# Edge stage of a graph network kernel: where the edge attribute maximum is found, how far the attribute products trail, and how cell rows are loaded

## The chip, the cores and the metric

The kernel runs on one core of one Trainium2 chip. The metric is the device time of one execution in microseconds; lower is better. Before the change it is 3320.58 us, the median of 3 runs (3318.75 to 3322.74).

## The reference, cut to what matters

Four graph layers work on 3125 nodes with 256 features and 50000 edges, each with 64 attributes and two weights. The change touches only what prepares the edges.

```
# layer 0, with h = batch-normalised x
a_in  = segment_sum((h @ W_in  + b_in )[src] * edge_weight[:, None],    dst)
a_out = segment_sum((h @ W_out + b_out)[dst] * edge_weight_n2[:, None], src)
# layer 1, three times
e_msg = edge_attr @ We[l].T + be[l]          # edge_attr: 50000 x 64
agg   = segment_sum(x[src] + e_msg, dst) / max(deg, 1)
x     = relu(agg @ Wl[l].T + bl[l] + x @ Wr[l].T)
# layers 2 and 3 use the same edges again, by products with the count matrix
```

Two things follow from the edges alone: a 3125 x 3125 matrix of cells (edge count and the two weight sums of each source and destination pair), and the sum of the edge attributes by destination.

## The kernel before, in words

The program is written out by hand, one instruction stream for each engine, joined by counting semaphores. An engine and its DMA queue run their instructions strictly in the written order, so what stands in a stream behind a waiting instruction waits too.

The 50000 edges are 391 tiles of 128 edges, in 49 chunks of 8 tiles (EC, CH). In time the part before the cell sweep is this.

1. **Zeroing and normalisation.** SyncE writes zeros over the cell matrix in HBM (39 stores of 3000 KB, L342). Beside it x is loaded, its column statistics are found and applied (DVE L1237 to L1253), and TensorE and ScalarE make the two 256-wide feature products, 25 node tiles, while ScalarE also stores the transposed features (hT_d, L550). DVE finds the largest and smallest feature values (L1261, L1262), makes the power-of-two scales (L1268 to L1276), and ScalarE and DVE split the features into two float16 parts (L569, L1283). The semaphore feat_split tells that this is done.
2. **Duplicate search.** Two edges of a tile that fall on one cell may not both be added by one indirect DMA. So ScalarE compares each tile's cells with three rows of cells that it loads broadcast from HBM (cell_rows, L577; L587, L595), 12 tiles ahead (AHEAD). TensorE decides which edge claims a cell (claim, L860) and adds up the values (sums, L870 to L875). DVE writes values and row numbers of a chunk (values, L1303 to L1306).
3. **Scatter.** For each tile GpSimd issues one indirect DMA that adds the values to the cell matrix (L505). It needs the whole matrix zeroed and the chunk's values ready; before the issue for tile t it waits for the landing of tile t-2. The values sit in VALS = 6 buffers.
4. **Attribute products.** For each tile DVE writes a one-hot of the destinations, 128 x 3125 in float16 (one_hot, L1318), into one of 3 buffers, and TensorE makes seven 500-column products with it (attributes, L884). The attributes are loaded by chunk (L361) and split into two float16 parts (attr_hi, attr_low). For the split their largest value must be known: 13 loads of 960 KB and a small one into two buffers, each read by two reductions of DVE (L1335, L1336), then a scale.

The tight loop of the last three runs in slots, one a tile (`for t in range(ET + LAG)` and its DVE and ACT counterparts). In slot t tile t is claimed and tile t - LAG has its attribute products, with LAG = EC * LAG_C, 48 slots before the change. The attribute maximum stands in DVE's stream at slot 37 (PEAK_SLOT) and its loads in SyncE's stream behind the zeroing and behind feat_split. The store of the normalised x (h_d, L353) also stands there, since the attribute chunks are loaded over its place in SBUF.

When the last scatter has landed (landed, L366) and the attribute sums are read out (s_ready), SyncE loads the first cells of the sweep (L373). From there on the change touches nothing.

Of the kernel before, what the change touches and what calls it, by code (L numbers as in the profile page):

```python
# [28 lines left out]
def build_gnn(nc, x, src, dst, edge_attr, edge_w, edge_w2, gamma0, beta0, W_in, b_in, W_out, b_out, W_x2i, b_x2i,  # L29
# [3 lines left out]
    E, EA = edge_attr.shape  # L33
# [22 lines left out]

    LAG_C = 6
    LAG = EC * LAG_C
    VALS = 6
    AHEAD = EC + 4  # L60
    PEAK_LOADS = 13
    PEAK_TILES = EM // PEAK_LOADS
    PEAK_SLOT, SCALE_SLOT = 37, 38

# [24 lines left out]
    with ExitStack() as ctx:  # L89
# [3 lines left out]
        def sem(name):  # L93
            return ctx.enter_context(nc.semaphore(name))
# [180 lines left out]
        peak_in = [sem(f"peak_in{s}") for s in range(2)]  # L275
        attr_in = [sem(f"attr_in{s}") for s in range(2)]
        landed = [sem(f"landed{s}") for s in range(2)]
        cells_in = [sem(f"cells_in{s}") for s in range(3)]
# [56 lines left out]
        def _(sp):  # L335
# [8 lines left out]

            sp.wait_ge(S["feat_split"], 2 * PIECES)
            for i in range(PEAK_LOADS):
                if i >= 2:
                    sp.wait_ge(S["peak_read"], i - 1)
                sp.dma_start(peak_buf[i % 2].rearrange("p (t a) -> p t a", a=EA), attr_main[:, i * PEAK_TILES:(i + 1) * PEAK_TILES, :]).then_inc(peak_in[i % 2], 16)
            sp.wait_ge(S["peak_read"], PEAK_LOADS - 1)  # L350
            sp.dma_start(peak_buf[PEAK_LOADS % 2][0:TAIL, 0:EA], edge_attr[EM * 128:E, :]).then_inc(peak_in[PEAK_LOADS % 2], 16)
            for lo, hi in ((0, K0), (K0, P)):
                sp.dma_start(by_node(h_d)[lo:hi], Xn[lo:hi]).then_inc(S["h_kept"], 16)  # L353
            sp.wait_ge(S["h_kept"], 32)
            for c in range(CH):
                if c >= 2:
                    sp.wait_ge(S["attr_lo"], c - 1)
                else:
                    sp.wait_ge(S["scale_a_ready"], 1)
# [110 lines left out]
        def _(pool):  # L470
# [21 lines left out]
            for q in (0, 32, 64):  # L492
                row = lambda b: brow[q + b:q + b + 1, 0:D]
                for a, v in ((row(0), b_in), (brow[q:q + 1, D:2 * D], b_out), (brow[q + 1:q + 2, :], b_x2i),
                             (row(2), bl[0]), (row(3), bl[1]), (row(4), bl[2]), (row(5), b_post)):
                    pool.dma_start(a, r1(v)).then_inc(S["bias_in"], 16)

            pool.wait_ge(S["zeroed"], 16 * (3 * CELLS // SLAB))
            for t in range(ET):
# [18 lines left out]
        def _(act):  # L518
# [53 lines left out]
            def load_rows(c):  # L572
                if c >= 2:
                    act.wait_ge(S["abs_done"], EC * (c - 1))
                a, b = max(EC * c - 1, 0), min(EC * c + EC + 1, ET)
                i_ = a - (EC * c - 1)
                act.dma_start(rows[c % 2][:, i_:i_ + b - a], cell_rows[a:b, :].unsqueeze(0).to_broadcast([128, b - a, 128])).then_inc(rows_in[c % 2], 16)  # L577
            for c in range(2):
                load_rows(c)

            def distance(t):
                c, k = divmod(t, EC)
                if k == 0:
                    act.wait_ge(rows_in[c % 2], 16 * (c // 2 + 1))
# [18 lines left out]
            def attr_hi(c):  # L603
                act.wait_ge(attr_in[c % 2], 16 * (c // 2 + 1) + (16 if c == CH - 1 else 0))
# [180 lines left out]
        def _(pe):  # L785
# [63 lines left out]
            pe.wait_ge(S["tr_read"], TR_AT["peak"])  # L849
            pe.matmul(trp[:, 0, 0:2], ident[0:1, 0:1].to_broadcast([1, 128]), power2[0:1, :], start=True, stop=True).then_inc(S["tr_done"], 1)  # L850

            def claim(t):
# [34 lines left out]
            for t in range(ET + LAG):  # L887
                if t == SCALE_SLOT + 1:
                    pe.wait_ge(S["tr_read"], TR_AT["peak2"])
                    pe.wait_ge(S["peak_a_ready"], 1)  # L890
                    pe.transpose(trp[0:1, 0, 0:128], peak_a, ident[:, :]).then_inc(S["tr_done"], 1)
                    pe.wait_ge(S["tr_read"], TR_AT["peak_a"])
                    pe.matmul(trp[:, 1, 0:1], ident[0:1, 0:1].to_broadcast([1, 128]), power_a[0:1, :], start=True, stop=True).then_inc(S["tr_done"], 1)
# [256 lines left out]
        def _(dve):  # L1150
# [103 lines left out]
            dve.wait_ge(S["stat"], 3)  # L1254

            for g in range(PIECES):
                dve.wait_ge(S["nat_ready"], NAT_AT["feat", (g + 1) * ROWS - 1])
# [18 lines left out]
            link(dve.tensor_scalar(scale0[:, 1:2], scale0[:, 1:2], ROOM, None, ALU.mult))  # L1276
            dve.sem_inc(S["scale0_ready"], 1)

            for n in range(2 * PIECES):
# [41 lines left out]
            for t in range(ET + LAG + EC):  # L1321
# [7 lines left out]
                if k == 5 and 1 <= c <= CH:  # L1329
                    values(c - 1)  # L1330
                if t == PEAK_SLOT:
                    for i in range(PEAK_LOADS + 1):
                        dve.wait_ge(peak_in[i % 2], 16 * (i // 2 + 1))
                        n, v = (128, peak_buf[i % 2]) if i < PEAK_LOADS else (TAIL, peak_buf[i % 2][0:TAIL, 0:EA])
                        dve.tensor_reduce(peaks_a[0:n, 0, i:i + 1], v, AX.X, ALU.max)  # L1335
                        last = dve.tensor_reduce(peaks_a[0:n, 1, i:i + 1], v, AX.X, ALU.min)  # L1336
                        last.then_inc(S["peak_read"], 1)
                    dve.wait_ge(S["peak_read"], PEAK_LOADS + 1)
                    link(dve.tensor_scalar(peaks_a[:, 1], peaks_a[:, 1], -1.0, None, ALU.mult))
                    dve.tensor_reduce(peak_a, peaks_a, AX.XY, ALU.max).then_inc(S["peak_a_ready"], 1)  # L1340
                if t == SCALE_SLOT:
                    dve.wait_ge(S["tr_done"], TR_AT["peak_a"])
                    dve.tensor_reduce(power_a[0:1, :], trp[0:1, 0, 0:128], AX.X, ALU.max).then_inc(S["tr_read"], 1)
                    dve.wait_ge(S["tr_done"], TR_AT["peak_a2"])
                    dve.tensor_scalar(power_a, trp[:, 1, 0:1], 2.0 ** -60, 2.0 ** 60, ALU.max, ALU.min).then_inc(S["tr_read"], 1)
                    dve.wait_ge(S["tr_read"], TR_AT["peak_a2"])
                    link(dve.tensor_scalar(power_a.bitcast(I32), power_a.bitcast(I32), 0x7F800000, None, ALU.bitwise_and))
                    link(dve.tensor_scalar(scale_a.bitcast(I32), power_a.bitcast(I32), -1.0, float(254 << 23), ALU.mult, ALU.add))
                    dve.tensor_scalar(unscale_a, power_a, 2.0 ** -14, None, ALU.mult)
                    link(dve.tensor_scalar(scale_a, scale_a, 2.0 ** 14, None, ALU.mult))  # L1350
                    dve.sem_inc(S["scale_a_ready"], 1)

# [240 lines left out]
```

## Time and profile before

| | |
|---|---|
| median of 3 runs | 3320.58 us |
| span of the profiled execution | 3315.2 us |
| median over the span of the profile | 5.4 us |
| zeroing of the cell matrix ends, first scatter | 352.66 us |
| first one-hot | 435.32 us |
| last scatter issued | 1183.19 us |
| first cell load of the sweep | 1243.72 us |

The times in the lower four lines count from the start of the span. PE is TensorE, ACT is ScalarE, POOL is GpSimd, SP is SyncE; an engine name with a q (SPq, ACTq) is the issue of DMAs by it. A releaser (`<-`) is what ended an idle time.

### The profile page before, as it was taken

To read this page: it belongs to the slowest core of one execution; us is meant where nothing else is said; L and a number is where in the kernel's file an instruction comes from. 1 tells how busy PE (TensorE), PEld (TensorE's weight loads), DVE (VectorE), ACT (ScalarE), POOL (GpSimd) and SP (SyncE) were. 2 spreads that over 40 slices of the span, in tenths; PEclk is the share of its full clock that TensorE was granted. 3 is DMA by queue.
4 is the path that set the end of the run, shared out by engine and by line. 5 is a ranking of instruction groups with operands and counts; after the bars stand their busy time and mean duration, and the time that the engine had idled before them with its cause. 6 is when DMAs were issued, how large, how long until landed. Compare 5 with 4: busy or idle time off the path is not lost. (4 is left out here: it accounts for less than half of the span.)

```text
span 3315.2 us, 37002 instructions
## 1 busy us (share of the span) xinstructions
PE 2562.0 (77%) x14593; PEld 1400.3 (42%) x14593; DVE 1677.6 (51%) x1848; ACT 1262.7 (38%) x2535; POOL 803.3 (24%) x611
## 2 busy tenths in 40 slices
PE   0551067777777777888888697998999978989896
PEld 0320033333333334444444443555555654555543
DVE  2540679999999994555545444102122242133313
ACT  0137067777777406666666422001011111122203
POOL 3000567777777722222222100000000000000000
PEclk9885589999999999999999898999999988999897
DMA  9999843333333309888898534534434424454362
GB/s 376 402 389 409 241 81 57 57 57 57 57 57 57 32 10 234 216 217 218 214 233 212 138 68 90 115 82 95 106 78 99 91 67 99 100 123 105 77 142 68
DMA packets 326008, 466.24 MB, mean 141 GB/s; under 512 B 106089, under 2 KB 261992, under 8 KB 325604
## 3 DMA queue, kind: packets, MB, share of 16 engines
q1 hardware_dynamic: 246445, 420.30, 46.9%
q0 software_dynamic: 57360, 0.92, 4.9%
q10 hardware_dynamic: 22023, 42.59, 4.0%
q8 instruction: 117, 1.92, 0.3%
q14 instruction: 63, 0.52, 0.1%
HBM read 313.97 MB, written 149.75 MB: 140 GB/s over the span
## 5 line engine op out<-in xcount | busy, mean ns | idle before, releaser
L1034 PE MATMUL psum<-FR 125*128 125x500 f16 (+1 forms) x4200 | 825.3, 355 | 40.9 <-DVE FR L1534 20.8
L505 POOL DMA_INDIRECT cell_mat<-ROW x391 | 619.6, 1585 | 536.3 <-DMA cell_mat<-SA 323.8
L884 PE MATMUL psum<-AR,Q 128*128 128x500 f16 (+1 forms) x2737 | 592.5, 356 | 184.0 <-DVE AR L1318 174.1
L1318 DVE TENSOR_SCALAR AR<-Q,ROW 128x3125 f16<-128x3125 f16 x391 | 721.4, 1902 | 7.0 <-PE psum L884 0.5
L1034 PEld LDWEIGHTS psum<-FR 125*128 125x128 f16 x4200 | 388.1, 98 | 451.8 <-issue 68.6
L884 PEld LDWEIGHTS psum<-AR,Q 128*128 128x128 f16 x2737 | 237.2, 98 | 455.5 <-DVE AR L1318 175.0
L1450 DVE SCALAR_TENSOR_TENSOR Q<-psum,small,ROW 128x1000 f32<-128x1000 f32 (+1 forms) x42 | 48.2, 1147 | 747.3 <-PE psum L1034 747.3
L1383 DVE SCALAR_TENSOR_TENSOR Q<-Q,small 125x1000 f16<-125x1000 f32 (+1 forms) x175 | 248.1, 1421 | 263.5 <-ACT Q L654 263.2
L654 ACT ACTIVATE Q<-Q,small 125x1000 f16<-125x1000 f32 (+1 forms) x175 | 262.2, 1499 | 116.7 <-DMA Q<-cell_mat 116.0
L928 PE MATMUL psum<-Q,FR 125*128 125x500 f16 (+1 forms) x1050 | 238.4, 365 | 77.9 <-DVE Q L1383 76.0
L982 PE MATMUL psum<-wl,Q 128*125 128x256 f32 (+1 forms) x1100 | 286.8, 401 | 5.7 <-ACT Q L700 3.0
L514 POOL CAST Q<-Q 125x500 f16<-125x500 f32 (+1 forms) x175 | 155.6, 890 | 550.2 <-DMA Q<-cell_mat 543.0
L587 ACT ACTIVATE AR<-AR,ROW 128x384 bf16<-128x384 f32 x391 | 235.0, 601 | 11.0 <-DMA AR<-cell_rows 10.6
L914 PE MATMUL psum<-Q,FR 125*128 125x500 f16 (+1 forms) x1050 | 210.7, 356 | 22.4 <-ACT Q L645 14.2
L982 PEld LDWEIGHTS psum<-wl,Q 128*125 128x125 f32 x1100 | 197.7, 188 | 62.4 <-issue 25.5
L645 ACT ACTIVATE Q<-psum 125x1000 f16<-125x1000 f16 (+1 forms) x175 | 159.8, 913 | 125.1 <-PE psum L914 95.5
L595 ACT ACTIVATE AR<-AR 128x384 bf16<-128x384 bf16 x391 | 198.7, 508 | 0.0
L627 ACT ACTIVATE ROW<-psum 128x1 f32<-128x1 f32 x391 | 64.9, 166 | 300.3 <-PE psum L860 289.4
L688 ACT ACTIVATE Q<-psum 128x1000 f32<-128x1000 f32 (+1 forms) x35 | 32.0, 915 | 377.1 <-PE psum L1061 377.1
L928 PEld LDWEIGHTS psum<-Q,FR 125*128 125x128 f16 x1050 | 91.9, 101 | 173.8 <-DVE Q L1383 89.8
L914 PEld LDWEIGHTS psum<-Q,FR 125*128 125x128 f16 x1050 | 93.8, 98 | 123.0 <-ACT Q L645 24.9
L629 ACT ACTIVATE ROW<-SA,ROW 128x9 bf16<-128x9 bf16 x391 | 119.1, 305 | 12.7
(271 smaller groups left out, 2321.4 us busy)
## 6 DMA issues: line engine op xcount, KB each, us to landing
cell_mat<-SA SPq DMA_DIRECT2D x39, 3000.0 KB, 31.7
Q<-cell_mat SPq DMA_DIRECT2D x150, 703.1 KB
FR<-count_mat SPq DMA_DIRECT2D x180, 585.9 KB
AR<-cell_rows ACTq DMA_DIRECT2D x47, 640.0 KB
count_mat<-Q SPq DMA_DIRECT2D x150, 117.2 KB
AR<-in_edge_attr SPq DMA_DIRECT2D x13, 960.0 KB, 4.7
Q<-in_edge_attr SPq DMA_DIRECT2D x48, 256.0 KB
cell_mat<-ROW POOLq DMA_INDIRECT x391
```

The lines of the kernel that those rows point to most:

```text
L505: pool.indirect_dma_start(out=cell_mat, out_offset=bass.IndirectOffsetOnAxis(ap=at[c % VALS][:, k:k + 1], axis=0), in_=vals[c % VALS][:, k ...
L587: act.activation(apart[t % 2].rearrange("p (j n) -> p j n", j=3), rows[c % 2][:, k:k + 3], ACT.Abs, bias=cell_neg[:, t:t + 1]).then_inc(S[ ...
L595: act.activation(same[c % 3][:, k], apart[t % 2].rearrange("p (j n) -> p j n", j=3), ACT.Relu, bias=1.0, scale=-1.0).then_inc(S["eq_done"], 1)
L645: act.activation(outw[:, 0:nt, :, tt * P:(tt + 1) * P], turn[n % 2][:, 0:nt], ACT.Copy).then_inc(S["turned"], 1)
L654: act.activation(split[n % 3][:, 0, :, 0:w], cells[n % 3][:, 0:3 * w].rearrange("p (n c) -> p c n", c=3)[:, 1:3], ACT.Copy, scale=scale0[0 ...
L884: last = pe.matmul(a, own_attr, onehot[t % 3][:, t0:t0 + nt], start=t == 0, stop=t == ET - 1, skip_group_check=True)
L914: last = pe.matmul(out_acc[:, hh, 0:ws], feat[1][:, t0 + k, c, f], outw[:, k, d, 0:ws], start=k == 0 and q == 0, stop=k == nt - 1 and q == ...
L928: pe.matmul(in_acc[:, hh, 0:w], feat[0][:, t, c, f], split[n % 3][:, d, 0, 0:w], start=t == 0 and q == 0, stop=t == NT - 1 and q == 2, ski ...
L982: last = pe.matmul(o, a[:, k * P:(k + 1) * P], wt, start=q == 0, stop=bias is None and q == len(ops) - 1)
L1034: last = pe.matmul(a[:, hh, 0:w], parts[:, c, t, f], slot(m, j)[:, i_, :], start=t == 0 and c == 0, stop=t == NT - 1 and c == 1, skip_grou ...
L1318: dve.tensor_scalar(onehot[t % 3], iota16, dst_c[:, t:t + 1], None, ALU.is_equal).then_inc(S["onehot_ready"], 1)
L1383: dve.scalar_tensor_tensor(out=split[n % 3][:, 1, :, 0:w], in0=cells[n % 3][:, 0:3 * w].rearrange("p (n c) -> p c n", c=3)[:, 1:3], scalar ...
```

## The change

It has five parts.

- The attribute maximum moves in DVE's stream from slot 37 to a place ahead of the feature maxima, right behind the input normalisation; its two buffers move from AR to FR. The scale that follows from it is made right behind the feature scales. ScalarE waits for the last of these reads before it writes the second half of the split features, which share FR.
- The 14 loads of the maximum, the store of h_d and the first 7 attribute chunk loads (EARLY) move from SyncE's stream to GpSimd's, ahead of the first scatter. SyncE keeps chunks 7 to 48, behind the zeroing. Chunk c from 2 on waits until chunk c-2 is split.
- LAG_C goes from 6 to 1: the attribute products trail the claims by 8 slots instead of 48.
- VALS goes from 6 to 14.
- Each chunk's cell rows come in three loads of 4, 3 and 3 rows (ROW_PARTS), issued at k = 1, 3 and 5 of the chunk before, instead of one load of 10 at k = 1.

```diff
-    LAG_C = 6
+    LAG_C = 1
-    VALS = 6
+    VALS = 14
-    PEAK_SLOT, SCALE_SLOT = 37, 38
+    EARLY = 7
+    ROW_PARTS = ((0, 4), (4, 7), (7, 10))
...
-        peak_buf = [AR[:, s * PEAK_TILES * EA:(s + 1) * PEAK_TILES * EA] for s in range(2)]
+        peak_buf = [FR[:, 6600 + s * PEAK_TILES * EA:6600 + (s + 1) * PEAK_TILES * EA] for s in range(2)]
... SyncE: these go
-            sp.wait_ge(S["feat_split"], 2 * PIECES)
-            for i in range(PEAK_LOADS):
...
-                sp.dma_start(by_node(h_d)[lo:hi], Xn[lo:hi]).then_inc(S["h_kept"], 16)
-            sp.wait_ge(S["h_kept"], 32)
-            for c in range(CH):
+            for c in range(EARLY, CH):
+                sp.wait_ge(S["attr_lo"], c - 1)
... GpSimd, ahead of the scatters
+            for i in range(PEAK_LOADS):
+                if i >= 2:
+                    pool.wait_ge(S["peak_read"], i - 1)
+                pool.dma_start(peak_buf[i % 2].rearrange("p (t a) -> p t a", a=EA), attr_main[:, i * PEAK_TILES:(i + 1) * PEAK_TILES, :]).then_inc(peak_in[i % 2], 16)
...
+            pool.wait_ge(S["feat_split"], 2 * PIECES)
+            for lo, hi in ((0, K0), (K0, P)):
+                pool.dma_start(by_node(h_d)[lo:hi], Xn[lo:hi]).then_inc(S["h_kept"], 16)
+            pool.wait_ge(S["h_kept"], 32)
+            for c in range(EARLY):
+                if c >= 2:
+                    pool.wait_ge(S["attr_lo"], c - 1)
+                pool.dma_start(attr32[c % 2], attr_main[:, EC * c:EC * c + EC, :]).then_inc(early_in[c % 2], 16)
... ScalarE
+                if n == PIECES:
+                    act.wait_ge(S["peak_read"], PEAK_LOADS + 1)
...
-                if k == 1 and 0 <= c + 1 < CH and c:
-                    load_rows(c + 1)
+                if k in (1, 3, 5) and c and c + 1 < CH:
+                    load_rows(c + 1, k // 2)
```

The streams show where things stand. First GpSimd's stream before, from the last bias row on (brow: bias rows; cell_mat<-ROW: the scatters; Q<-Q: casts of the sweep).

```order
L496 DMA brow<-in_L_gnn_bl 1x16x16 x3
L496 DMA brow<-in_L_gnn_b_post 1x16x16
L505 DMA cell_mat<-ROW 9984000x3 x391
L514 CAST Q<-Q 125x500 x150
L514 CAST Q<-Q 125x125 x25
```

And the same place now.

```order
L485 DMA brow<-in_L_gnn_b_post 1x16x16
L490 DMA FR<-in_edge_attr 128x1920 x13
L492 DMA FR<-in_edge_attr 80x64
L495 DMA h_d<-Q 120x25x256
L495 DMA h_d<-Q 5x25x256
L500 DMA Q<-in_edge_attr 128x512 x7
L509 DMA cell_mat<-ROW 9984000x3 x391
```

Twenty-three DMAs stand ahead of the first scatter; the last nine of them wait for feat_split, and of these five also for the split of earlier attribute chunks.

Next DVE's stream where the claims begin. Before (L1294: the mask of earlier edges; L1303 to L1306: values of a chunk; L1335: the first read for the attribute maximum):

```order
L1283 SCALAR_TENSOR_TENSOR FR<-AR,small,FR 125x5x256 x10
L1287 MEMSET AR 128x128
L1294 TENSOR_TENSOR Q<-AR,ROW 128x1024 x2
L1303 TENSOR_REDUCE ROW<-ROW 128x24
L1304 SCALAR_TENSOR_TENSOR ROW<-ROW 128x8
L1305 TENSOR_TENSOR ROW<-ROW 128x8
L1306 TENSOR_TENSOR ROW<-ROW 128x8
L1294 TENSOR_TENSOR Q<-AR,ROW 128x1024
```

Now (L1342: the split of an attribute chunk; L1348: one-hots):

```order
L1313 SCALAR_TENSOR_TENSOR FR<-AR,small,FR 125x5x256 x10
L1317 MEMSET AR 128x128
L1324 TENSOR_TENSOR Q<-AR,ROW 128x1024
L1342 SCALAR_TENSOR_TENSOR Q<-Q,small 128x8x64
L1324 TENSOR_TENSOR Q<-AR,ROW 128x1024
L1348 TENSOR_SCALAR AR<-Q,ROW 128x25x125 x5
L1342 SCALAR_TENSOR_TENSOR Q<-Q,small 128x8x64
L1348 TENSOR_SCALAR AR<-Q,ROW 128x25x125
L1333 TENSOR_REDUCE ROW<-ROW 128x24
```

The second instruction of the loop now needs the first attribute chunk, and one-hots begin before the values of chunk 0 are written.

## Rows read from the trace of the kernel before

**Rows 1.** Page, costliest groups of instructions: busy us, mean ns | idle before.

```profile
L505 POOL DMA_INDIRECT cell_mat<-ROW x391 | 619.6, 1585 | 536.3 <-DMA cell_mat<-SA 323.8
L1318 DVE TENSOR_SCALAR AR<-Q,ROW 128x3125 f16<-128x3125 f16 x391 | 721.4, 1902 | 7.0 <-PE psum L884 0.5
```

**Rows 2.** Stretches: window, length, busy PE, PEld, DVE, ACT, POOL, clock, DMA share, GB/s.

```profile
250.00:300.00 50.00, 6.54 (x97) 4.56 (x97) 4.05 (x12) 43.06 (x122) 0.00 (x0) 0.50 1.02 409
350.00:400.00 50.00, 0.00 (x0) 0.00 (x0) 42.39 (x21) 0.00 (x0) 32.58 (x21) 0.50 0.72 194
600.00:700.00 100.00, 76.37 (x528) 38.92 (x528) 98.70 (x85) 70.83 (x206) 75.60 (x47) 1.00 0.37 57
```

**Rows 3.** Timeline of the edge stage: start, us, engine, what [idle before <-releaser].

```profile
352.66 1.69 POOL L505 DMA_INDIRECT cell_mat<-ROW  x1 [323.76 <-DMA cell_mat<-SA]
409.04 9.15 SPq L353 DMA_DIRECT2D h_d<-Q  x2
429.59 4.64 SPq L361 DMA_DIRECT2D Q<-in_edge_attr  x3
432.37 0.72 ACT L610 ACTIVATE Q<-Q,small 128x512 f16<-128x512 f32 x1 [11.17 <-DMA Q<-in_edge_attr]
435.32 3.71 DVE L1318 TENSOR_SCALAR AR<-Q,ROW 128x3125 f16<-128x3125 f16 x2
1183.19 1.55 POOL L505 DMA_INDIRECT cell_mat<-ROW  x1 [0.30 <-issue]
1243.72 2.34 SPq L373 DMA_DIRECT2D Q<-cell_mat  x6
```

**Rows 4.** Stretches of the scatters alone (L505), then of the last values (L1306).

```profile
604.60:1108.20 503.60, 382.24 (x240) 1.00 0.36 56
1108.20:1184.80 76.60, 60.28 (x39) 1.00 0.29 19
...
615.10:1113.80 498.70, 5.04 (x30) 1.00 0.36 56
```

**Rows 5.** Timeline of one chunk's scatters and its cell row load.

```profile
612.01 2.02 POOL L505 DMA_INDIRECT cell_mat<-ROW  x1 [0.30 <-issue]
614.34 1.55 POOL L505 DMA_INDIRECT cell_mat<-ROW  x1 [0.30 <-issue]
617.50 1.54 POOL L505 DMA_INDIRECT cell_mat<-ROW  x1 [1.62 <-DMA cell_mat<-ROW]
...
612.16 0.33 ACTq L577 DMA_DIRECT2D AR<-cell_rows  x1
```

**Rows 6.** Start of the program: timeline of PE, then of DVE.

```profile
72.34 1.97 PE L799 MATMUL psum<-ident,AR 128*128 128x128 f32 x8 [54.15 <-DMA AR<-in_L_gnn_We]
133.67 6.82 DVE L1253 TENSOR_TENSOR Q<-Q,FR 125x6400 f32<-125x6400 f32 x1
229.17 0.17 DVE L1264 TENSOR_SCALAR small<-small 125x10 f32<-125x10 f32 x1
248.71 0.17 DVE L1287 MEMSET AR<- 128x128 f32 x1
```

**Rows 7.** Groups by line, DVE, windows 0:400 (first) and 140:250.

```profile
L1335 DVE TENSOR_REDUCE small<-AR 128x1 f32<-128x1920 f32 x11 | 23.7, 2152 | 45.2 <-DMA AR<-in_edge_attr 44.9
...
L1261 DVE TENSOR_REDUCE small<-AR 125x1 f32<-125x1280 f32 x10 | 14.8, 1481 | 60.3 <-ACT AR L560 60.3
```

**Rows 8.** DMA, window 60:80: packets, MB, share by queue (q1 SyncE, q10 ScalarE).

```profile
q1 hardware_dynamic: 1687, 6.61, 80.1%
q10 hardware_dynamic: 1687, 1.66, 23.5%
```

**Rows 9.** DMA issues, windows 0:352 and 350:412: KB each, us from issue to landing.

```profile
cell_mat<-SA SPq DMA_DIRECT2D x39, 3000.0 KB, 31.7
FR<-in_L_gnn_gamma POOLq DMA_DIRECT2D x1, 125.0 KB, 6.9
...
AR<-in_edge_attr SPq DMA_DIRECT2D x11, 960.0 KB, 4.7
```

More of the change, by code:

```diff
@@ L276, in build_gnn @@
         attr_in = [sem(f"attr_in{s}") for s in range(2)]
+        early_in = [sem(f"early_in{s}") for s in range(2)]
         landed = [sem(f"landed{s}") for s in range(2)]
@@ L496, in _ @@
                     pool.dma_start(a, r1(v)).then_inc(S["bias_in"], 16)
+            for i in range(PEAK_LOADS):
+                if i >= 2:
+                    pool.wait_ge(S["peak_read"], i - 1)
+                pool.dma_start(peak_buf[i % 2].rearrange("p (t a) -> p t a", a=EA), attr_main[:, i * PEAK_TILES:(i + 1) * PEAK_TILES, :]).then_inc(peak_in[i % 2], 16)
+            pool.wait_ge(S["peak_read"], PEAK_LOADS - 1)
+            pool.dma_start(peak_buf[PEAK_LOADS % 2][0:TAIL, 0:EA], edge_attr[EM * 128:E, :]).then_inc(peak_in[PEAK_LOADS % 2], 16)
+            pool.wait_ge(S["feat_split"], 2 * PIECES)
[6 more added lines that the diff above has]
+                pool.dma_start(attr32[c % 2], attr_main[:, EC * c:EC * c + EC, :]).then_inc(early_in[c % 2], 16)
             pool.wait_ge(S["zeroed"], 16 * (3 * CELLS // SLAB))
@@ L568, in _, with load_rows @@
                 now = slice(g * ROWS, (g + 1) * ROWS)
+                if n == PIECES:
+                    act.wait_ge(S["peak_read"], PEAK_LOADS + 1)
                 act.activation(feat[b][:, now, 0], Bn[b][:, now], ACT.Copy, scale=scale0[0:P, 0:1]).then_inc(S["feat_hi"], 1)
             act.wait_ge(S["feat_split"], 2 * PIECES)
-            def load_rows(c):
+            def load_rows(c, part):
                 if c >= 2:
                     act.wait_ge(S["abs_done"], EC * (c - 1))
-                a, b = max(EC * c - 1, 0), min(EC * c + EC + 1, ET)
-                i_ = a - (EC * c - 1)
-                act.dma_start(rows[c % 2][:, i_:i_ + b - a], cell_rows[a:b, :].unsqueeze(0).to_broadcast([128, b - a, 128])).then_inc(rows_in[c % 2], 16)
+                first = EC * c - 1
+                a, b = max(first + ROW_PARTS[part][0], 0), min(first + ROW_PARTS[part][1], ET)
+                act.dma_start(rows[c % 2][:, a - first:b - first], cell_rows[a:b, :].unsqueeze(0).to_broadcast([128, b - a, 128])).then_inc(rows_in[c % 2], 16)
             for c in range(2):
-                load_rows(c)
+                for part in range(len(ROW_PARTS)):
+                    load_rows(c, part)
             def distance(t):
@@ L583, in distance @@
                 if k == 0:
-                    act.wait_ge(rows_in[c % 2], 16 * (c // 2 + 1))
+                    act.wait_ge(rows_in[c % 2], 16 * len(ROW_PARTS) * (c // 2 + 1))
                 if t >= 2:
@@ L603, in attr_hi @@
             def attr_hi(c):
-                act.wait_ge(attr_in[c % 2], 16 * (c // 2 + 1) + (16 if c == CH - 1 else 0))
+                if c < EARLY:
+                    act.wait_ge(early_in[c % 2], 16 * (c // 2 + 1))
+                else:
+                    act.wait_ge(attr_in[c % 2], 16 * len(range(EARLY + (c - EARLY) % 2, c + 1, 2)) + (16 if c == CH - 1 else 0))
                 if c >= 2:
@@ L850, in _ @@
             pe.matmul(trp[:, 0, 0:2], ident[0:1, 0:1].to_broadcast([1, 128]), power2[0:1, :], start=True, stop=True).then_inc(S["tr_done"], 1)
+            pe.wait_ge(S["tr_read"], TR_AT["peak2"])
+            pe.wait_ge(S["peak_a_ready"], 1)
+            pe.transpose(trp[0:1, 0, 0:128], peak_a, ident[:, :]).then_inc(S["tr_done"], 1)
+            pe.wait_ge(S["tr_read"], TR_AT["peak_a"])
+            pe.matmul(trp[:, 1, 0:1], ident[0:1, 0:1].to_broadcast([1, 128]), power_a[0:1, :], start=True, stop=True).then_inc(S["tr_done"], 1)
             def claim(t):
@@ L887, in _ @@
             for t in range(ET + LAG):
[L888 to L893, printed above, removed]
                 if 1 <= t <= ET:
@@ L1254, in _ @@
             dve.wait_ge(S["stat"], 3)
+            for i in range(PEAK_LOADS + 1):
+                dve.wait_ge(peak_in[i % 2], 16 * (i // 2 + 1))
+                n, v = (128, peak_buf[i % 2]) if i < PEAK_LOADS else (TAIL, peak_buf[i % 2][0:TAIL, 0:EA])
+                dve.tensor_reduce(peaks_a[0:n, 0, i:i + 1], v, AX.X, ALU.max)
+                last = dve.tensor_reduce(peaks_a[0:n, 1, i:i + 1], v, AX.X, ALU.min)
+                last.then_inc(S["peak_read"], 1)
+            dve.wait_ge(S["peak_read"], PEAK_LOADS + 1)
+            link(dve.tensor_scalar(peaks_a[:, 1], peaks_a[:, 1], -1.0, None, ALU.mult))
+            dve.tensor_reduce(peak_a, peaks_a, AX.XY, ALU.max).then_inc(S["peak_a_ready"], 1)
             for g in range(PIECES):
@@ L1277, in _ @@
             dve.sem_inc(S["scale0_ready"], 1)
+            dve.wait_ge(S["tr_done"], TR_AT["peak_a"])
+            dve.tensor_reduce(power_a[0:1, :], trp[0:1, 0, 0:128], AX.X, ALU.max).then_inc(S["tr_read"], 1)
+            dve.wait_ge(S["tr_done"], TR_AT["peak_a2"])
+            dve.tensor_scalar(power_a, trp[:, 1, 0:1], 2.0 ** -60, 2.0 ** 60, ALU.max, ALU.min).then_inc(S["tr_read"], 1)
+            dve.wait_ge(S["tr_read"], TR_AT["peak_a2"])
+            link(dve.tensor_scalar(power_a.bitcast(I32), power_a.bitcast(I32), 0x7F800000, None, ALU.bitwise_and))
+            link(dve.tensor_scalar(scale_a.bitcast(I32), power_a.bitcast(I32), -1.0, float(254 << 23), ALU.mult, ALU.add))
+            dve.tensor_scalar(unscale_a, power_a, 2.0 ** -14, None, ALU.mult)
+            link(dve.tensor_scalar(scale_a, scale_a, 2.0 ** 14, None, ALU.mult))
+            dve.sem_inc(S["scale_a_ready"], 1)
             for n in range(2 * PIECES):
@@ L1330, in _ @@
                     values(c - 1)
[L1331 to L1351, printed above, removed]
             dve.wait_ge(S["attr_done"], ET)
```

10 lines of the change are left out of this document (removed).

## The prediction

> **What bounds the kernel now.** I read the page's groups first, then the stretches, then the timelines of the edge stage. The two costliest groups outside the layers are GpSimd's scatters and DVE's one-hots [rows 1]; both belong to the stage ahead of the cell sweep. The stretches show three phases [rows 2]. Until 352.66 the DMA engines are full (share 1.02 in 250:300) while DVE has 4 us of work in 50. In 350:400 DVE reads the attributes for their maximum, PE and ACT do nothing. From 435 on DVE is busy 98.7 us of 100, in one chunk of 8 slots every 16.62 us (30 chunks in 498.7 us [rows 4]), 2.077 us a slot. The stage's end is set by DVE: the first one-hot starts at 435.32, the last scatter is issued at 1183.19, and the sweep's first cell load comes only at 1243.72, when the attribute sums are out [rows 3]. So 60 us of slack separate the scatters from the end.
>
> A second bound lies close behind. The scatters take 240 issues in 503.6 us, 2.098 us each [rows 4], a hair slower than DVE's 2.077: GpSimd has values waiting and goes at its own pace. An issue costs 1.55 + 0.30 = 1.85 us; the rest is once a chunk, beside the cell row load of 612.16: one issue of 2.02 instead of 1.55, and an idle of 1.62 until the scatter two back has landed [rows 5]. In the last 39, with little other traffic (19 GB/s against 56), it is 76.6/39 = 1.96 [rows 4].
>
> **Start of the claims (first part).** The maximum is read right after DVE's normalisation, which ends at 133.67 + 6.82 = 140.5 [rows 6]. The first two loads now run beside the weight loads that PE waits for until 72.34 [rows 6]. With two queues at work each gets the same number of packets, 1687 and 1687 in 20 us [rows 8]; per engine that is 105 rounds, 190 ns a round, and (6.61 + 1.66) MB/20 us = 26 bytes/ns an engine. A load of 960 KB is 128 partition rows of 7680 B, 8 per engine. Two loads put 16 packets of 295 ns ahead of the weights: +5 us, DVE is ready at 145.
>
> One load under the zeroing takes 8 rounds of (4000 + 7680)/26 = 449 ns, 3.6 us and a fixed part: gamma, 8 packets of 1000 B an engine, landed in 6.9 us on this very queue, and its rounds make 1.5 [rows 9], so 5 us. That is 8.6 us against 4.7 without the zeroing [rows 9]. Both buffers turn in 8.6 + two reductions of 2.15 with 0.3 for hand-over, 13.1 us for two loads [rows 7]. The thirteenth is read by 145 + 4.3 + 6 x 13.1 = 228. Then 20 feature reductions of 1.48 [rows 7], at most 30 us, 28 as each starts before the last is through: the feature maxima are done at 257 instead of 229.2. From there to the split's end it took 19.5 us before (229.17 to 248.71 [rows 6]), and the attribute scale adds 2.5: 279. The 28 us are paid under the zeroing, by nobody but the claims.
>
> **Store of h_d and first attribute chunk (second part).** Chunk 0 may only come when h_d is stored. The store has 3000 packets of 1 KB on 15 engines, 200 each; it was issued at 409.04 and SyncE, which waited for it, went on at 429.59; less the fixed part some 17 us of data, 84 ns a packet, with only scatters beside it [rows 3]. Beside zeroing each packet waits for one of 4000 B, 154 ns: 200 x 238 = 48 us, or 200 x 193 = 39 us if bytes alone count. I take 43, and 5 fixed: 327. GpSimd must also write 3000 descriptors; from the 128 of a scatter in 1.55 us that is at most 12 ns each, 36 us, and hides in the transfer; laid end to end it would cost 30 more. Chunk 0 lands 7 us later (8 rounds of 233 ns and 5), at 334. ACT's attr_hi to the first one-hot took 3 us (432.37 to 435.32 [rows 3]); with the four slots still to claim I take 7: **first one-hot at 341**, 94 us earlier. The claims stand still at slot 3 from about 285 to 334, and no longer run 36 slots ahead under the zeroing. That is the price of LAG 8, and the reason that not all of the time gets through.
>
> **DVE's path.** From slot 8 on nothing leaves DVE's work: the same 391 one-hots and 49 masks and splits. 391 slots of 2.077 = 812 us: attribute sums out at 341 + 812 + 3 = 1156. Values of the last chunk (slot 397) at 341 + 389 x 2.077 = 1149, seven scatters of 1.85 and a landing of about 3: 1166.
>
> **GpSimd's path (second and fourth part).** The zeroing ended at 352.66 with the engines full. 12.8 MB for the maximum at 409 GB/s [rows 2] are 31 us, h_d 10 to 17, seven attribute loads 4.5: 402. GpSimd's last early load (chunk 6) waits for the split of chunk 4 in slot 36, 341 + 28 x 2.077 = 399. Both let the scatters start at 402. VALS = 14 holds 112 tiles; at 402 DVE has written 24, so it doesn't bind.
>
> **Cell rows in three (fifth part).** A load of 640 KB becomes 256, 192 and 192. Per chunk of 8 issues the ideal is 14.8 us and the actual one 16.79; 2.0 us are the row and attribute loads' doing. The stall is what a load delays a landing beyond its slack of about 0.7 us, so smaller pieces hide better: I take 0.5 for the first part, which meets the attribute load, and 0.1 for the others. The longer issue (up to 0.47) came when ACT's issue met the start of GpSimd's; with three issues a chunk I take 3 x 0.17 = 0.5, and 0.15 of rest. 14.8 + 1.25 = 16.05 a chunk, **2.00 a tile**. Ends: 1.88 (nothing left but traces) and 2.10 (no gain). ACT's new limit, the third part landing before the next chunk's first comparison three slots later (6.2 us), isn't reached: even the whole 640 KB had let the scatters go 5.3 us after its issue [rows 5]. A miss would cost each chunk what lies beyond 6.2.
>
> GpSimd: 402 + 391 x 2.00 + 3 = **1187**. That is later than DVE's 1166, and so the new end.
>
> **A rule against the move.** Scatters take 1.55 us beside a DVE that is 98.7% busy with one-hots, and 1.54 at 617.50 as well as 1.69 at 352.66 before any one-hot [rows 2, 3, 5]. By the Trainium skill (SBUF — State Buffer, Who interferes with whom) a DVE instruction in a two-port mode locks GpSimd out, and a DMA issued from GpSimd then waits for its descriptors; moving 23 DMAs there would make each wait for up to a one-hot, 1.9 us. By that rule six early loads would cost at most 11 us of GpSimd's time; the trace doesn't show it for scatters, and the reads of the maximum are reductions.
>
> **The sum.** The first cell load goes from 1243.7 to 1187, -57. PE now idles some 40 us ahead of the sweep instead of 10; at 350:400 an idle PE stood at clock 0.50 [rows 2], so the first tiles run slow: +2. Nothing later moves. 3315.2 - 55 = 3260 of the profiled execution; the median lay 5.4 above its span, so 3265.
>
> **The rivals.**
> - *DVE stays the bound.* The three loads hide fully, the pace is under 1.95, and DVE's 1166 decides: -77, 3245. For it: 1.85 in every undisturbed stretch. Against: three issues a chunk instead of one, and 1.96 in the nearly undisturbed tail. 20%.
> - *The split of the row loads does nothing.* The bytes are the same and the pace stays 2.10: 402 + 821 + 3 = 1226, -16 with the clock, 3305. The same time results if h_d is late by 30 and the pace 2.02. 22%.
> - *GpSimd's queue starves beside the zeroing (slower).* The place is the 13 loads of the maximum. I have no row of a large load on this queue; a store of the zeroing takes 31.7 us to land [rows 9]. If a load takes that, two turn in 36.3: the maximum at 367, features split at 418, and with the zeroing over by then h_d needs 22: first one-hot at 455. The scatters can't start before slot 36, at 513, and end at 513 + 782 + 3 = 1298: +54, 3375. The point from which it is slower is a first one-hot after 397, that is 18 us a load instead of 8.6. Against it: the 31.7 hold several stores queued behind each other, and gamma landed in 6.9. 8%.
> - *The change does not take the maximum off the path*: DVE reads it while it would idle anyway, but h_d and the attributes come out so late that the first one-hot is at 390 to 400: within 0.2%. 4%.
>
> My forecast, GpSimd bound with a pace of 1.95 to 2.06: 46%. For a range of 8 in 10: 3238 (DVE bound, h_d by bytes) to 3312 (old pace and 6 us more). 0.2% is 6.6 us, about what a measurement of this kernel can tell. Faster: 46 + 20 + 21 = 87%; same 5%; slower 8%.
>
> **What would show it.** Right: first one-hot near 341; first scatter near 402, released by the zeroing; mean spacing 2.00 with landing waits under 1 us; first cell load near 1187 with DVE done some 30 us before. Wrong: reads of the maximum more than 7 us apart a load; GpSimd waiting for values rather than landings at the end (DVE bound); a first scatter released by an attribute load well after 402; DVE below 98% busy in the loop, which would mean rows or attributes come late.

## The result, and the profile after

The changed kernel takes 3291.58 us, the median of 4 runs (3289.40 to 3295.41), against 3321.66 (3318.75 to 3322.76, 4 runs) of the kernel before: a ratio of 0.9913, 95% interval 0.9901 to 0.9925. The forecast was 3265 with a range of 3238 to 3312. The sign, the range and the bound that was named (GpSimd) held; the pace of the scatters did not get better as forecast, and the gain is 30 us, where 56 were forecast.

The profiled execution is the longest of the four, 3295.41 us, with a span of 3293.4. First its two groups from the page (busy, mean ns | idle before), which answer to [rows 1], then the edge stage's timeline, put together by engine: GpSimd, DVE, PE, SyncE (start, us, what [idle before <-releaser]), which answers to [rows 3, 6].

```profile
L1348 DVE TENSOR_SCALAR AR<-Q,ROW 128x3125 f16<-128x3125 f16 x391 | 722.4, 1902 | 9.2 <-PE psum L899 1.5
L509 POOL DMA_INDIRECT cell_mat<-ROW x391 | 610.4, 1561 | 211.4 <-DMA cell_mat<-ROW 110.8
```

```profile
281.80 2.32 POOL L495 DMA_DIRECT2D h_d<-Q  x2 [57.45 <-DVE FR L1313]
313.92 1.16 POOL L500 DMA_DIRECT2D Q<-in_edge_attr  x2 [29.81 <-DMA h_d<-Q]
...
388.56 0.54 POOL L500 DMA_DIRECT2D Q<-in_edge_attr  x1 [16.08 <-DVE Q L1342]
397.18 1.68 POOL L509 DMA_INDIRECT cell_mat<-ROW  x1 [8.08 <-DMA cell_mat<-SA]
...
1209.30 1.55 POOL L509 DMA_INDIRECT cell_mat<-ROW  x1 [0.30 <-issue]
...
139.02 6.82 DVE L1262 TENSOR_TENSOR Q<-Q,FR 125x6400 f32<-125x6400 f32 x1
...
230.79 2.14 DVE L1269 TENSOR_REDUCE small<-FR 128x1 f32<-128x1920 f32 x1
...
261.51 0.17 DVE L1283 TENSOR_SCALAR small<-small 125x10 f32<-125x10 f32 x1
...
281.59 0.17 DVE L1317 MEMSET AR<- 128x128 f32 x1
...
326.04 3.71 DVE L1348 TENSOR_SCALAR AR<-Q,ROW 128x3125 f16<-128x3125 f16 x2
...
1142.51 0.34 DVE L1364 TENSOR_SCALAR SA<-psum,small 128x125 f32<-128x125 f32 x1
...
1223.53 1.09 PE L948 MATMUL psum<-ident,Q 125*125 125x125 f16 x8 [82.23 <-DVE Q L1392]
...
1213.86 2.44 SPq L362 DMA_DIRECT2D Q<-cell_mat  x6
```

Read it from the end. DVE has put the attribute sums out at 1142.9; the last scatter is issued at 1209.30, and the first cell load at 1213.86, where it was 1243.72: 29.9 us earlier. (The medians differ by 30.1, but the spans of these two profiles only by 21.8: behind the first cell load the changed one takes 8.0 us more. The part on the sweep below comes back to that.) GpSimd now ends the stage, DVE 66 us ahead of it. The first one-hot came 109 us earlier than before, the last scatter 26 us later: the kernel before had 60 us between last scatter and first cell load, the changed one has 4.6.

Where the scatters' time goes shows in GpSimd's waits between 450 and 1130, first of the kernel before and then of the changed one (what it waited for: us, times, longest). A landing wait is idle time of GpSimd that ends when an earlier scatter has landed (`<- DMA cell_mat<-ROW`).

```profile
POOL cell_mat L505 <- issue: 83.6, 264, 1.2
POOL cell_mat L505 <- DMA cell_mat<-ROW: 80.4, 62, 3.3
```

```profile
POOL cell_mat L509 <- DMA cell_mat<-ROW: 101.8, 87, 2.6
POOL cell_mat L509 <- issue: 74.3, 236, 1.2
```

The "issue" part is the fixed 0.30 us between two issues. The rest is waiting for the landing of the scatter two back: shorter at the worst (2.6 for 3.3 us) but in 87 places instead of 62, and in sum more. Each landing wait holds the fixed 0.30 us too; above it they are 101.8 - 87 x 0.30 = 75.7 us, where the kernel before had 80.4 - 62 x 0.30 = 61.8. One place looks like this (GpSimd's scatters, then ScalarE's loads of cell rows, then SyncE's load of attributes), beside [rows 5]:

```profile
702.90 1.56 POOL L509 DMA_INDIRECT cell_mat<-ROW  x1 [0.34 <-issue]
704.77 1.55 POOL L509 DMA_INDIRECT cell_mat<-ROW  x1 [0.30 <-issue]
708.29 1.55 POOL L509 DMA_INDIRECT cell_mat<-ROW  x1 [1.97 <-DMA cell_mat<-ROW]
...
703.62 0.33 ACTq L583 DMA_DIRECT2D AR<-cell_rows  x1
707.81 0.33 ACTq L583 DMA_DIRECT2D AR<-cell_rows  x1
...
704.10 0.33 SPq L350 DMA_DIRECT2D Q<-in_edge_attr  x1
```

and the attribute load of the kernel before that belongs to [rows 5]:

```profile
612.64 0.33 SPq L361 DMA_DIRECT2D Q<-in_edge_attr  x1
```

The load of 703.62 is the first of its chunk, 256 KB, and the attribute load of another 256 KB goes out 0.5 us behind it. The landing wait that follows is 1.97 us, where the whole 640 KB of 612.16, with its attribute load also 0.5 us behind it, had 1.62 [rows 5]. So the smaller first piece doesn't make this wait shorter. The second load, at 707.81, is followed by none.

### The profile page after: what moved, and what is told of

The parts are those of the page before. It is cut to its first block and busy times, and to the rows that moved or that the text cites. A ratio compares the mean times of both kernels' runs of the same rounds, so it can differ in the third digit from the quotient of the medians.

```text
span 3293.4 us, 37092 instructions
## 1 busy us (share of the span) xinstructions
PE 2569.1 (78%) x14593; PEld 1405.8 (43%) x14593; DVE 1676.6 (51%) x1848; ACT 1267.4 (38%) x2535; POOL 805.8 (24%) x634
## 5 line engine op out<-in xcount | busy, mean ns | idle before, releaser
L1348 DVE TENSOR_SCALAR AR<-Q,ROW 128x3125 f16<-128x3125 f16 x391 | 722.4, 1902 | 9.2 <-PE psum L899 1.5
L509 POOL DMA_INDIRECT cell_mat<-ROW x391 | 610.4, 1561 | 211.4 <-DMA cell_mat<-ROW 110.8
L948 PE MATMUL psum<-ident,Q 125*125 125x125 f16 x1250 | 104.2, 226 | 82.2 <-DVE Q L1392 82.2
L937 PEld LDWEIGHTS psum<-Q,FR 125*128 125x128 f16 x1050 | 93.0, 102 | 172.6 <-DVE Q L1392 88.0
L948 PEld LDWEIGHTS psum<-ident,Q 125*125 125x125 f16 x1250 | 101.8, 143 | 112.4 <-issue 85.3
```

Of the source, the lines that this page charges most:

```text
L509: pool.indirect_dma_start(out=cell_mat, out_offset=bass.IndirectOffsetOnAxis(ap=at[c % VALS][:, k:k + 1], axis=0), in_=vals[c % VALS][:, k ...
L937: pe.matmul(in_acc[:, hh, 0:w], feat[0][:, t, c, f], split[n % 3][:, d, 0, 0:w], start=t == 0 and q == 0, stop=t == NT - 1 and q == 2, ski ...
L948: last = pe.transpose(turn[n % 2][:, k, c], split[n % 3][:, c, 1, k * P:(k + 1) * P], ident16[0:P, 0:P])
L1348: dve.tensor_scalar(onehot[t % 3], iota16, dst_c[:, t:t + 1], None, ALU.is_equal).then_inc(S["onehot_ready"], 1)
```

## The experiments

The theory after the result: the stage ends with GpSimd's scatters, DVE's path is free by 66 us, and the pace fell short because three row loads a chunk disturb more scatters than one. Rivals: DVE still decides, through the values; the lag or the early loads brought the gain; the attribute loads hold the scatters up; the missing microseconds lie in the cell sweep.

All paces below are counted in one window, 520 to 1070, in which every kernel scatters all the time. The view is the stretch 520:1070 with the scatters' line alone (length, busy, count, clock, DMA share, GB/s).

**One row load a chunk again.** Run twice, the second time on the same chip as a repeat of the changed kernel.

```diff
-    ROW_PARTS = ((0, 4), (4, 7), (7, 10))
+    ROW_PARTS = ((0, 10),)
-                if k in (1, 3, 5) and c and c + 1 < CH:
+                if k == 1 and c and c + 1 < CH:
```

> The changed kernel with one row load a chunk (10 rows) instead of three. Changed kernel: 320 scatters beside the loads took 684 us, 2.137 us each, the last 70 1.86. Theory of the prediction (smaller pieces hide): the pace goes back to 2.20 or more, the time rises by 15 to 30 us. Rival 1 (a load costs a stall whatever its size): the pace falls to 2.10 or below, the time falls by 8 to 15 us. Rival 2 (only the bytes count): pace and time stay within 3 us.

> The changed kernel with one row load a chunk, a second time, on the same chip as the changed kernel itself. The pace of the scatters was 2.086 with one load against 2.136 with three, 264 x 0.05 = 13 us less for the middle of the run, of which 6 us were seen in the median. Theory that three loads cost: 4 to 8 us below the changed kernel again. Rival (spread of the runs): no difference.

> The changed kernel unchanged, to compare with on the same chip: 3290 to 3293 us, pace 2.13 to 2.14.

Measured: 3285.68 us (3276.35 to 3290.03), ratio 0.9886 (0.9868 to 0.9904); again 3286.45, 0.9898 (0.9881 to 0.9915). The changed kernel repeated: 3291.56, 0.9914 (0.9897 to 0.9931). The first cell load stands at 1206.81 and 1204.24, against 1213.86 and 1216.00. In the window 264 scatters instead of 259 (first the changed kernel, then one row load):

```profile
520.00:1070.00 550.00, 404.12 (x259) 1.00 0.39 57
```

```profile
520.00:1070.00 550.00, 424.08 (x264) 1.00 0.37 57
```

With one load the issues are longer (424.08/264 = 1.61 us against 404.12/259 = 1.56), as [rows 5] had shown, but the landing waits between 450 and 1130 are only 68.7 us in 55 places:

```profile
POOL cell_mat L509 <- issue: 87.3, 273, 1.7
POOL cell_mat L509 <- DMA cell_mat<-ROW: 68.7, 55, 2.5
```

ScalarE's queue between 450 and 1130 (packets, MB, share of the engines), first of the changed kernel, then with one load:

```profile
q10 hardware_dynamic: 16416, 24.78, 13.9%
```

```profile
q10 hardware_dynamic: 5472, 24.78, 11.1%
```

The bytes are the same 24.78 MB, the packets a third. The split of the row loads costs 5 to 6 us both times. The intervals of the two kernels' ratios still overlap, but in the second comparison, on one chip, all four times with one load (the highest 3288.59) lie below all five of the changed kernel (the lowest 3289.31), and the counts of scatters and the place of the first cell load say the same. **The change without the split is the fastest complete kernel here**, level with its two variants further below (3286.38 and 3286.98).

Which of the three loads costs it can be counted from GpSimd's timeline. Each landing wait above 0.30 between 520 and 1070 (33 chunks) is put down to the row load that was issued last before the wait began. In the changed kernel that makes 1.2 us a chunk behind the first load (with the attribute load beside it), 0.1 behind the second and 0.7 behind the third, 2.0 in all (1.1, 0.1 and 0.7 in its repeat); with one load it is 1.4, in the kernel before 1.5.

**Five row loads a chunk.**

```diff
+    ROW_PARTS = ((0, 2), (2, 4), (4, 6), (6, 7), (7, 10))
+                if 1 <= k <= 5 and c and c + 1 < CH:
+                    load_rows(c + 1, k - 1)
```

> The changed kernel with five row loads a chunk (2, 2, 2, 1 and 3 rows) at k = 1 to 5. The same bytes in more pieces. Prediction's theory: pace under 2.10, time down by 10 us or more. A stall for each load: pace 2.2 or more, time up by 20 us or more. Bytes alone: no change.

Measured: 3292.08 us, ratio 0.9911 (0.9896 to 0.9926); 258 scatters in the window, first cell load 1217.36; the landing waits 114.1 us in 121 places. From three to five loads the scatters hardly get slower. The landing waits look as if they went on growing, from 101.8 us, but 34 more places hold the fixed 0.30 us each, 10.2 us, which stood under "issue" before; above it they are 77.8 us against 75.7. Both theories that expected 10 us or 20 us of change are out; "bytes alone" fits this pair, but not the step from one load to three.

**The kernel before with three row loads.** The row loads' part of the change alone.

> The kernel before with three row loads a chunk instead of one, nothing else. Its stage ends with the one-hots, 60 us after the last scatter, so every theory expects the same time within 0.2%; it is the pace of the scatters (before 2.098 from 604.6 to 1108.2) that tells. Prediction: 2.00. A stall for each load: 2.14 or more, and the 60 us of slack shrink by 15 us. Bytes alone: 2.10.

Measured: 3320.64 us, ratio 1.0000 (0.9990 to 1.0009). The scatters fell from 263 to 259 in the window and the last was issued at 1192.62 instead of 1183.19, without an effect on the time: they had 60 us of slack. The part is a loss that shows only where scatters decide.

**No attribute loads from chunk 7 on.** The loads of chunks 7 to 48 and their waits are left out, so the products of those chunks use old attributes.

> The changed kernel without the attribute loads of chunks 7 to 48; these chunks use the attributes left in the buffers, so this part of the result is left out. It splits the excess of 0.29 us a tile over 1.85 between row loads and attribute loads. If the stall goes by loads (three of rows, one of attributes), the pace falls by a quarter of 0.29 to about 2.07; if it goes by bytes (262 of 917 KB), to 2.06; if the attribute load matters most because it meets the first row load, to 2.00 or less. Time: 320 tiles times the fall, down by 20 to 45 us, with the one-hots the next bound 70 us earlier.

Measured in one run: 3276.84 us, first cell load at 1203.37; 265 scatters in the window, at 41 GB/s instead of 57. So the attribute loads cost about as much as the split does, six scatters in 550 us (0.05 us a tile), and not the bulk of what lies above 1.86. The landing waits behind the three row loads are 0.5, 0.4 and 0.9 us a chunk here.

**VectorE blocked for 41 us.** The same 20 maxima in the changed kernel and in the kernel before.

```diff
+                if t == 300:
+                    for i in range(20):
+                        dve.tensor_reduce(peaks_a[0:P, i % 2, i // 2:i // 2 + 1], FR[0:P, 6600:6600 + PEAK_TILES * EA], AX.X, ALU.max)
```

> The changed kernel with 20 more maxima over 1920 values (2.15 us each, 43 us together) on VectorE at slot 300 of the edge stage; their results are not used. GpSimd theory: VectorE is some 66 us ahead of the scatters (its last work of the stage at 1143, the last scatter at 1209), so the 43 us are hidden: last scatter 1206 to 1213, total within 5 us of the changed kernel's 3291.6. If VectorE is what bounds the stage: about 3334. A third answer, in between, would be a gain of a few us from a shorter idle time of TensorE before the sweep (82 us there, some 40 here).

> The kernel before with the same 20 maxima at slot 300. Its scatters stand on the heels of VectorE (values come when VectorE has made them), so the 43 us should be seen: 3320.6 + 43 = 3364, less what GpSimd's queue holds as a lead by slot 300. By the lead of the buffers, at most six chunks deep, a rival says that they are partly hidden: 3330 to 3350.

Measured: changed 3293.69 us (3287.36 to 3294.16), ratio 0.9910 (0.9893 to 0.9926); before 3362.59 (3362.49 to 3364.56), 1.0125 (1.0108 to 1.0142). The same 41.3 us of DVE work cost the kernel before 41 us and the changed one about 2, which its runs can't tell from nothing. Here are the block in the changed kernel, the sums out, the last scatter and the first cell load:

```profile
936.20 41.27 DVE L1355 TENSOR_REDUCE small<-FR 125x1 f32<-125x1920 f32 x20
...
1185.30 0.34 DVE L1367 TENSOR_SCALAR SA<-psum,small 128x125 f32<-128x125 f32 x1
...
1211.12 1.55 POOL L509 DMA_INDIRECT cell_mat<-ROW  x1 [0.30 <-issue]
...
1214.77 2.63 SPq L362 DMA_DIRECT2D Q<-cell_mat  x6
```

and the same end in the kernel before, where DVE's last sums and not the last scatter release it:

```profile
1216.59 1.54 POOL L505 DMA_INDIRECT cell_mat<-ROW  x1 [0.30 <-issue]
...
1285.09 0.34 DVE L1358 TENSOR_SCALAR SA<-psum,small 128x125 f32<-128x125 f32 x1
...
1285.93 2.22 SPq L373 DMA_DIRECT2D Q<-cell_mat  x6
```

The expectation for the kernel before had the size right and the reason wrong. It looked to values that come late for the scatters, less a lead of the buffers; but the last scatter stands 69 us ahead of the first cell load here too, and nothing is hidden, since DVE itself ends the stage with the attribute sums. The block also shows the scatters alone, as PE and ACT had nothing to do and loaded nothing (the stretch with all engines: busy PE, PEld, DVE, ACT, POOL, clock, DMA share, GB/s):

```profile
942.60:977.85 35.25, 0.00 (x0) 0.00 (x0) 35.25 (x18) 0.00 (x0) 29.41 (x19) 0.50 0.22 1
```

19 scatters in 35.25 us, 1.855 each, in the middle of the stage. This is 1.55 + 0.30 and no wait at all; what lies above it beside the loads is the loads' work, or that of the engines which stand still with them.

**Six chunks of lag again, with one row load.**

```diff
-    LAG_C = 1
+    LAG_C = 6
```

> The changed kernel with one row load a chunk and the attribute products six chunks behind again (LAG_C = 6), VALS still 14. Under the zeroing the claims then don't stand at slot 3 but run on to slot 36 or so while h_d is stored. If the lag carries the gain, the time goes back towards that of the kernel before. My theory: the scatters set the end; first scatter 397 plus 1.6 us for each of five chunks of rows now loaded before it, about 405; the last row load comes 40 slots (83 us) earlier, so 83 us more run at 1.88 instead of 2.09 a tile, -8. Both cancel: within 4 us of the same kernel with LAG_C = 1 (3286).

The expectation failed: 3312.29 us (3309.24 to 3315.66), ratio 0.9976 (0.9965 to 0.9986), 26 us more than with a lag of one. The pace is the same, 266 in the window. GpSimd's timeline shows where it began:

```profile
414.65 0.54 POOL L500 DMA_DIRECT2D Q<-in_edge_attr  x1 [16.08 <-DVE Q L1342]
431.27 0.54 POOL L500 DMA_DIRECT2D Q<-in_edge_attr  x1 [16.08 <-DVE Q L1342]
432.12 1.68 POOL L509 DMA_INDIRECT cell_mat<-ROW  x1 [0.31 <-issue]
```

GpSimd works in order. Its seventh early load waits for the split of chunk 4, which with the long lag comes at 431, and the scatters stand behind it, though the zeroing had long been over. I had looked at what DVE and the buffers would do and not at that queue.

**The same with two early loads instead of seven.** This was to tell whether the lag or the queue cost the 26 us. The edit is against the changed kernel; row loads are one a chunk as well.

```diff
-    LAG_C = 1
+    LAG_C = 6
-    EARLY = 7
+    EARLY = 2
```

> One row load, attribute products six chunks behind again, and only the first two attribute loads on GpSimd's queue (the others on SyncE's). If the 26 us that six chunks of lag cost with seven early loads came from GpSimd waiting in its own order for loads 2 to 6, the first scatter is back at 397 to 403, the last at 1200 to 1208, and the time is that of lag one with one row load, 3286 (3281 to 3292). If the lag itself costs (VectorE or TensorE later by five chunks of products), the time stays near 3310.

Measured: 3286.38 us (3279.99 to 3288.52), ratio 0.9888 (0.9871 to 0.9904).

```profile
317.72 1.16 POOL L500 DMA_DIRECT2D Q<-in_edge_attr  x2 [32.08 <-DMA h_d<-Q]
401.45 1.68 POOL L509 DMA_INDIRECT cell_mat<-ROW  x1 [82.57 <-DMA cell_mat<-SA]
```

The queue was the cause. With it free, a lag of six takes the same time as a lag of one: DVE is done at 1183.5 instead of 1143, and that is still before the scatters. So, with 14 value buffers, the lag of one brings nothing by itself; it only keeps seven early loads on GpSimd from delaying the scatters. This kernel is also nearly the first two parts of the change alone: against the kernel before it has the maximum, the store of h_d and two attribute loads moved, and the 14 buffers.

**Scatters into 512 rows only.** Every target is a spill row, so the cell matrix stays empty. This was to be a control for the row loads' part.

> The changed kernel with all scatters sent to the 512 spill rows instead of their cells; the cell matrix stays empty, so the sums over it are left out of the result. It is the control for the same kernel without row loads. If random rows of 117 MB of HBM make the landings slow, the pace falls below 2.05; if only the loads beside them do, it stays at 2.13 to 2.15.

It failed as a control, and neither of the two paces that were expected came: one run of 3475.13 us, 198 scatters in the window, 2.78 us each, landing waits of 273.0 us in 174 places between 450 and 1130. The issues are as short as ever (mean 1563 ns on the page), so all of it is landing. It says that the place of the targets matters for the landing, and nothing on the row loads.

**TensorE kept busy before the sweep, with one row load.** 168 matmuls without use, four behind each of the last landings and 28 behind the very last.

```diff
+            for i in range(36):
+                t = ET - 36 + i
+                pe.wait_ge(landed[t % 2], 16 * (t // 2 + 1))
+                for _ in range(4 if t < ET - 1 else 28):
+                    pe.matmul(psum[0:P, 4, 0:4 * P]..., ident16[0:P, 0:P], ident16[0:P, 0:P]..., start=True, stop=True)
```

> One row load, and 168 matmuls of 500 columns whose results nobody uses on TensorE while the last 36 scatters run and just after, in what were 82 idle us before the sweep. If the idle TensorE (clock 0.72 in 1100:1200, 0.84 in 1200:1300) is what makes the sweep give back some 3.5 us in its first 20 tiles, the time falls from 3286 to 3280 to 3284. If that loss has another cause (the loads of the cells), it stays at 3286; if the extra matmuls delay the first turn of the sweep, it rises by the same few us.

Measured: 3286.98 us (3284.80 to 3288.50), ratio 0.9894 (0.9877 to 0.9910). Stretches of the kernel with one row load and an idle TensorE, then of this one (columns as in [rows 2]):

```profile
1100.00:1200.00 100.00, 33.02 (x203) 15.53 (x201) 41.94 (x38) 10.10 (x33) 83.27 (x55) 0.73 0.24 1
1200.00:1300.00 100.00, 71.10 (x440) 38.14 (x441) 41.62 (x28) 56.06 (x44) 28.35 (x27) 0.90 0.88 216
```

```profile
1100.00:1200.00 100.00, 68.42 (x336) 31.75 (x336) 43.17 (x38) 11.31 (x36) 81.28 (x54) 0.98 0.23 1
1200.00:1300.00 100.00, 82.94 (x474) 44.30 (x473) 40.75 (x27) 55.37 (x43) 26.63 (x26) 0.93 0.86 211
```

The granted clock rose from 0.73 to 0.98 before the sweep, but only from 0.90 to 0.93 in the first 100 us of it, and the time didn't move. From first cell load to the span's end it is 3286.3 - 1208.18 = 2078.1 us, against 3284.8 - 1206.81 = 2078.0 with one row load and an idle TensorE. At the sweep's start PE waits for DVE, DVE for ScalarE and ScalarE for the loads of the cells (in the changed kernel until 1223.53, 1221.84 and 1220.19), so a slow clock there is hidden.

## Why the prediction was right, and where its sizes were off

**The mechanism** was the forecast's own case: reading the maximum beside the zeroing takes DVE off the end of the stage, the scatters start when the zeroing ends and then decide. The blocked DVE shows the last part directly. That the moved maximum (with its loads and the store of h_d) is what brings the gain follows from the runs: the row loads' part gives nothing or costs 5 us, the lag gives nothing once the queue is free, and the kernel that has neither of them takes 3286.38 us. The number of value buffers was not varied. By the timelines DVE's values are at most 5.25 chunks ahead of the scatters in the changed kernel, which six buffers would have held, and 7.0 with the long lag, which they would not.

The forecast's own case was narrower, though: "GpSimd bound with a pace of 1.95 to 2.06". The bound came true and the pace didn't. Of the times that it named, the rival "the split of the row loads does nothing" (3305) is off by 13 us and the forecast (3265) by 27. That the measured time lies in the range is owed to its upper end, the old pace and 6 us more.

**The start of the claims**, step by step: DVE ready for the maximum at 145.8 (forecast 145); loads of the maximum landing in 9.2 us (8.6); the last big one read at 232.9 (228); feature maxima 261.5 (257); split out 281.6 (279). All within 5 us, though no row had shown a large load on this queue beside the zeroing. The rival in which GpSimd's queue starves had its point at 18 us a load; it is out.

**The store of h_d** went out at 281.80, and chunk 0 was issued at 313.92: 32 us against a forecast of 48, and below both of its bounds (39 and 48 for the data alone). Per engine 200 packets in at most 32 us are 160 ns each, where I had put a whole zeroing packet of 154 ns in front of each and 84 ns for itself. The first one-hot was therefore at 326 and not 341. It gained nothing, as DVE isn't the bound. The same holds for the 36 us that 3000 descriptors might have cost GpSimd: its two issues took 2.32 us.

**First scatter** 397.2 against 402, released by the zeroing; the last early load had gone at 388.6 (399). The wait that I had weighed by the Trainium skill (SBUF — State Buffer, Who interferes with whom) is not seen here: with DVE busy 19.78 of the 20 us from 380 to 400, the early load of 388.56 took 0.54 us to issue, and from 310 to 397 GpSimd's seven loads of 256 KB landed 7.4 us after their issue in the median, ScalarE's six of 256 KB 7.5. Whether the one-hots run in a two-port mode at all, of which that rule speaks, no run shows, so it is not refuted. The price of these loads was the in-order wait, 26 us with the long lag, which I had only as "last early load 399".

**The step that was mis-sized is the pace.** Forecast 2.00 us a tile with three row loads, from 2.098; measured 550/259 = 2.12, and over the whole run (1209.3 - 397.2)/390 = 2.08, because the last 63, behind the last landing wait of 1092.09, run undisturbed at 1.86. 0.08 x 391 is 31 us, less 5 for the earlier start: that is the 27 us by which the first cell load missed 1187. My term was "smaller pieces hide better": it took a landing to be delayed in step with the load's bytes, less a slack of about 0.7 us, which left 0.5 us of landing wait a chunk for the first part and 0.1 for each of the others. Measured (between 520 and 1070) they are 1.2, 0.1 and 0.7. The longer issues went the other way: they were 0.4 us a chunk before, I let them grow to 0.5, and with three loads they are 0.1.

| us a chunk of 8 scatters | before | forecast | changed | one load |
|---|---|---|---|---|
| landing waits above 0.30 | 1.5 | 0.7 | 2.0 | 1.4 |
| issues longer than 1.55 | 0.4 | 0.5 | 0.1 | 0.5 |

The sum itself had a slip as well: 0.5 + 0.1 + 0.1 + 0.5 + 0.15 is 1.35 and not 1.25, which makes 2.02 a tile instead of 2.00, and some 7 us more. The rival "the split does nothing" had the pace nearly right for the stage's middle (2.10 for 2.12), and none of the undisturbed tail.

**The sweep** was to give back 2 us by a slow clock. By the profiles it is 2079.5 us from first cell load to the end, against 2071.5 before. Part of these 8 us is the choice of execution: the profiled one of the changed kernel took 3.8 us more than its median (3295.41 against 3291.58), and the span of the kernel before, 3315.2, with the 1.8 us by which its later times exceed their spans, lies some 5 us below its median of 3321.66. The two kernels with the blocked DVE are a fairer pair, as both profiles lie within 0.5 us of their medians: 2077.1 for the changed one, 2075.0 for the kernel before. So about 2 us are given back, the size that was forecast, but their cause stays open. The clock is not shown to be it, since the warmed TensorE didn't bring them back. As far as the runs show, that the number fits is luck.

**What stays open.** Why a scatter beside loads lands late, by the number of packets or by the number of loads, was not separated: the runs changed both together. Neither explains by itself why the second of three loads costs 0.1 us and the third, of the same 192 KB, 0.7. And the kernel lets only two scatters be under way, because the duplicate search covers neighbouring tiles only; with a third the landing waits might go altogether, which wasn't tried.

## What to carry to other kernels

When a long wait goes, price the second bound by its own rows and not by what it might become: the scatters stood 60 us from the end at 2.10 a tile, and 402 + 391 x 2.10 + 3 = 1226 for the first cell load (measured 1213.86) was nearer than the 1187 of an improved pace. Splitting a transfer need not divide the harm that it does to a short one beside it: here it rose from 1.4 to 2.0 us a chunk. And when work is put on an engine's queue ahead of a stage, look at what that engine's next instruction waits for: a load of half a microsecond's issue held 391 scatters back by 30 us.

## What the runs showed of the hardware

- Scatters of 128 rows of three values from GpSimd, at most two under way: 1.855 us each alone. Beside 57 GB/s of loads: 2.08 (one row load a chunk), 2.12 (three), 2.13 (five). With all targets in 512 rows: 550/198 = 2.78.
- A plain store of 3125 packets of 1 KB, in two DMAs, takes GpSimd 2.32 us to issue and is landed 32 us after the first issue, beside the full zeroing.
- A load of 960 KB from GpSimd's queue lands in 9.2 us beside the zeroing; from SyncE's queue without it 4.7 [rows 9].
- TensorE's granted clock of 0.73 or 0.98 in the 100 us ahead of a stage that waits for its loads made no difference to that stage.
